# Weighted aggregation of a graph-attention layer: own rows added to source rows before the segment product

## The reference

```python
s_all = jnp.concatenate([src, loops])
d_all = jnp.concatenate([dst, loops])
...
alpha = p / z[d_all]
agg = jax.ops.segment_sum(alpha[:, :, None] * v[s_all], d_all, num_segments=n)
agg = jnp.where(deg[:, None, None] > 0, agg, jnp.zeros_like(agg))
att = agg.reshape(n, NH * HD) @ Wo + bo
x = residual + att
```

## Time and profile before

| | us |
|---|---|
| median of 3 runs (2486.36 to 2490.35) | 2487.27 |
| span of the profiled execution | 2872.0 |
| of it, the stage `weighted` | 365 (from 1745 to 2110) |
| TensorE busy | 2193.6 |
| VectorE busy | 1930.2 |
| ScalarE busy | 1328.2 |
| GpSimd busy | 1228.6 |

### The profile page before, as it was taken

How to read it: one execution, slowest core, us unless ns; L and a number is a source line. 1 busy time by engine, 2 the same in 40 slices (tenths; PEclk the granted TensorE clock), 3 DMA queues, 4 the chain that set the end, 5 groups by cost and what they waited for, 6 DMA issues and landing times. The chain is left out here.

```text
span 2872.0 us, 49421 instructions
## 1 busy us (share of the span) xinstructions
PE 2193.6 (76%) x14363; PEld 1777.0 (62%) x14363; DVE 1930.2 (67%) x7755; ACT 1328.2 (46%) x3166; POOL 1228.6 (43%) x1416
## 2 busy tenths in 40 slices
PE   2478777548887677728888806878849999999998
PEld 2355555348887566715656606777737777777776
DVE  3589999736665577736666694444547777777775
ACT  0489999712222244436656600000015656656655
POOL 3544434146652666445455103555543333333332
PEclk9789999879998899958888857888969999999999
DMA  3478888668775466624333104445432333333331
GB/s 92 133 213 244 243 239 250 178 184 232 232 229 175 125 197 199 185 94 119 110 119 117 58 9 116 131 145 153 130 123 83 106 111 104 106 111 102 108 111 49
DMA packets 354022, 413.95 MB, mean 144 GB/s; under 512 B 51578, under 2 KB 235278, under 8 KB 353754
## 3 DMA queue, kind: packets, MB, share of 16 engines
q1 hardware_dynamic: 316186, 340.50, 37.9%
q0 software_dynamic: 34496, 69.37, 9.1%
q10 hardware_dynamic: 3072, 0.92, 0.1%
HBM read 264.11 MB, written 179.90 MB: 155 GB/s over the span
## 5 line engine op out<-in xcount | busy, mean ns | idle before, releaser
L1746 PEld LDWEIGHTS p_y<-w,g_T 128*128 128x128 f32 x3136 | 365.4, 192 | 46.4 <-issue 24.2
L1746 PE MATMUL p_y<-w,g_T 128*128 128x128 f32 x3136 | 365.8, 275 | 0.0
L1764 ACT ACTIVATE nT<-p_n 128x512 f32<-128x512 f32 x98 | 58.5, 597 | 644.8 <-PE p_n L1754 644.8
L1739 PE MATMUL p_f<-nT,w 128*128 128x512 f32 x784 | 354.4, 595 | 0.0
L548 POOL DMA_INDIRECT x_dst<-in_x_dram,idx x196 | 189.0, 964 | 283.0 <-DMA edge_x<-x_dst 200.4
L1729 POOL TENSOR_TENSOR rstd<-var,minus_half 128x4 f32<-128x4 f32 x98 | 113.4, 1157 | 450.1 <-ACT res L1777 450.0
L1771 ACT ACTIVATE g_T<-p_f,bf 128x512 f32<-128x512 f32 x392 | 267.1, 681 | 31.5 <-PE p_f L1739 31.4
L1131 POOL DMA_INDIRECT x_src<-x_rows,idx x196 | 185.1, 944 | 210.5 <-ACT normed L1219 113.9
L1550 POOL DMA_INDIRECT x_rows<-xv,idx x196 | 197.3, 1007 | 160.5 <-DVE xv L1636 104.4
L902 POOL DMA_INDIRECT h_src<-h_table,idx x196 | 192.4, 982 | 156.2 <-POOLq L123 57.2
L894 POOL DMA_INDIRECT e_h<-in_x_dram,idx x172 | 168.3, 979 | 178.8 <-DVE msg L1010 78.4
(11 more groups left out here) (309 smaller groups left out, 5874.0 us busy)
## 6 DMA issues: line engine op xcount, KB each, us to landing
xs<-x_rows SPq DMA_DIRECT2D x98, 512.0 KB, 3.6
x_in<-in_x_dram SPq DMA_DIRECT2D x98, 256.0 KB
h_table<-h_rows SPq DMA_DIRECT2D x98, 256.0 KB
x_rows<-x_in SPq DMA_DIRECT2D x98, 256.0 KB, 2.9
out_dram<-res SPq DMA_DIRECT2D x98, 256.0 KB, 2.1
x_rows<-x_rows SPq DMA_DIRECT2D x50, 500.0 KB
edge_x<-x_dst SPq DMA_DIRECT2D x98, 128.0 KB
h_own<-edge_x SPq DMA_DIRECT2D x49, 256.0 KB
```

Of the source, the lines that this page charges most:

```text
L1739: e.matmul(p_f[ch][:], w_1[:, ch * P:(ch + 1) * P], nT[:, g % 2, :], start=True, stop=True).then_inc(f_prod, 1)
L1746: mm = e.matmul(p_y[g % 2][:, a * D:(a + 1) * D], g_T[:, g % 2, ch, a * P:(a + 1) * P], w_2[:, ch, :], start=(ch == 0), stop=(ch == FCH - 1))
```

## The change

The own rows are added to the source rows before the segment product, so one product of a tile does for two: the four identity products of a group are gone. VectorE gets a new addition for each group, `w_sum` plus `w_own`, both in SBUF, with a semaphore `weight_ready` of its own. An own row now goes through `mate` too and reaches every column of its segment, and through the carries the next tiles; so it must count once in a segment, and its weight is multiplied by `end_t` in place of `done_t`: 1 at the last edge of a segment alone. `end_t` is a value that `prepare` made before without keeping it, and is written to a tile of its own.

The carries move from lag 4 to lag 5, `p_out` from lag 5 to lag 6, the last sum from lag 6 to lag 7; OUT goes from AHEAD + 4 to AHEAD + 5, so there is one step more. Loads, scatters and the numbers of buffers stay.

```diff
-                    chain(e.tensor_tensor(tmp[:], tmp[:], real[:], ALU.mult))
-                    chain(e.scalar_tensor_tensor(out=tmp[:], in0=dst_f[:], scalar=-float(SKIP), in1=tmp[:],
+                    chain(e.tensor_tensor(end_t[:], tmp[:], real[:], ALU.mult))
+                    chain(e.scalar_tensor_tensor(out=tmp[:], in0=dst_f[:], scalar=-float(SKIP), in1=end_t[:],
...
-                    chain(e.tensor_tensor(top[:], top[:], over_heads(done_t), ALU.mult))
+                    chain(e.tensor_tensor(top[:], top[:], over_heads(end_t), ALU.mult))
...
-                OUT = AHEAD + 4
+                OUT = AHEAD + 5
...
                         if at_step(n, AHEAD + 1):
                             g = n - AHEAD - 1
-                            e.wait_ge(src_ready, g + 1)
                             e.wait_ge(mate_ready, g + 1)
-                            e.wait_ge(own_ready, g + 1)
+                            e.wait_ge(weight_ready, g + 1)
                             wait(e, attT_ready, GT * (g - 1))
                             for j in range(GT):
                                 at = slice(j * P, (j + 1) * P)
-                                e.matmul(p_att[g % 2][:, at], w_src[:, g % 2, j, :], mate[:, g % 2, at], start=True, stop=False)
-                                mm = e.matmul(p_att[g % 2][:, at], w_own[:, g % 2, j, :], ident[:], start=False, stop=True)
+                                mm = e.matmul(p_att[g % 2][:, at], w_sum[:, g % 2, j, :], mate[:, g % 2, at], start=True, stop=True)
...
-                        if at_step(n, AHEAD + 2):
-                            g = n - AHEAD - 2
+                        if at_step(n, AHEAD + 3):
+                            g = n - AHEAD - 3
...
+                    for n in range(STEPS):
+                        carried, weighed = at_step(n, AHEAD + 2), at_step(n, AHEAD)
+                        if carried:
+                            carry(n - AHEAD - 2, 0)
...
+                        if weighed:
+                            e.wait_ge(own_ready, g + 1)
+                            e.wait_ge(src_ready, g + 1)
+                            e.tensor_tensor(w_sum[:, g % 2, :, :], w_sum[:, g % 2, :, :], w_own[:, g % 2, :, :], ALU.add).then_inc(weight_ready, 1)
+                        if at_step(n, AHEAD + 4):
+                            g = n - AHEAD - 4
```

More of the change, by code:

```diff
@@ L179, in gnn_program @@
         done_col = sb("done_col", [P, T])
-        done_t = sb("done_t", [Q, W])
+        end_t = sb("end_t", [Q, W])
         same_prev = sb("same_prev", [Q, W])
@@ L211, in prepare @@
                 seg_f = sb("seg_f", [Q, W], F32, c)
+                done_t = sb("done_t", [Q, W], F32, c)
                 norm_f = sb("norm_f", [Q, W], F32, c)
@@ L1466, in weighted @@
                 mate = sb("mate", [P, 2, GROUP], F32, c)
-                w_src = sb("w_src", [P, 2, GT, D], F32, c)
+                w_sum = sb("w_sum", [P, 2, GT, D], F32, c)
                 w_own = sb("w_own", [P, 2, GT, D], F32, c)
@@ L1490, in weighted @@
                 own_ready = sem("own_ready", c)
+                weight_ready = sem("weight_ready", c)
                 att_prod = sem("att_prod", c)
@@ L1596, in _ @@
                 def _(e):
-                    for n in range(STEPS):
[L1598 to L1629, removed]
-                                                seg_col[:, g * GT:(g + 1) * GT].rearrange("p (q c) -> p q c", q=2)
-                                                .unsqueeze(3).to_broadcast([P, 2, 2, P]), ALU.is_equal).then_inc(mate_ready, 1)
-                            if j == 3 and at_step(n, AHEAD + 3):
-                                g = n - AHEAD - 3
-                                e.wait_ge(out_prod, g + 1)
-                                e.wait_ge(xv_in[g % VN], 16 * (g // VN + 1))
-                                e.tensor_tensor(xv[:, g % VN, :, X2, :], p_out[g % 2][:].rearrange("p (j d) -> p j d", j=GT),
-                                                xv[:, g % VN, :, X1, :], ALU.add).then_inc(row_ready, 1)
@@ new lines, in carry @@
+                    def carry(g, j):
+                        t = g * GT + j
+                        at = slice(j * P, (j + 1) * P)
+                        e.wait_ge(att_prod, g + 1)
+                        wait(e, out_prod, g - 1)
+                        if t == 0:
+                            e.tensor_copy(attT[:, 0, at], p_att[0][:, at]).then_inc(attT_ready, 1)
+                            return
+                        e.wait_ge(attT_ready, t)
+                        s, end = (t - 1) // GT % 2, (t - 1) % GT * P + P - 1
+                        e.scalar_tensor_tensor(out=attT[:, g % 2, at], in0=tile_row(rows[:, g % RN, :, :], j, FROM_PREV - SEG),
+                                               scalar=attT[:, s, end:end + 1], in1=p_att[g % 2][:, at],
+                                               op0=ALU.mult, op1=ALU.add).then_inc(attT_ready, 1)
```

27 lines of the change are left out of this document (added).

## The result

The change makes the kernel slower by a little: 2491.26 us (median of 6 runs, 2486.76 to 2497.22) against 2486.82 us of the kernel before (6 runs beside them). The ratio is 1.0023, with a 95% interval of 1.0013 to 1.0033, so +5.7 us, between 3 and 8. A repeat beside other kernels gave 1.0021 (1.0011 to 1.0030). The forecast of 2486 us, no measurable change, had the range right and the sign wrong.

A forecast was written before the change was run, and what follows sets the result against it. The prediction took GpSimd's scatters to bound the stage `weighted`, so removed products and added work were worth 0; 2487.3 - 1.5 + 1 = 2486.8, put at 2486 us, with a range of 2462 to 2500.

The forecast's parts named there:

- What sets the pace: In stage `weighted`, GpSimd's scatters set the timed stage, at about 280 us; chance 0.62.
- The budget of stages: Timed total less the other stages' floors leaves 263 to 306 us for `weighted`; GpSimd's own floor there is 278.
- the 15 long waits: VectorE's carries in `weighted` wait 93.5 us in 15 long pieces; mostly late completions belonging to the profiled execution.
- The step prices: Per group in `weighted`: GpSimd 5.16 us; TensorE 4.98 falling to 4.08; VectorE 3.4 rising to 4.0.
- the loop: In `weighted`, `mate`, `p_att`, carry 0 and back to `mate` take 4.98 us; as rival pacing the stage, 2469 us, chance 0.24.
- cover: GpSimd's 5.16 us a step hides TensorE's saving in `weighted`: worth 0, or 44 us if not hidden.
- The fill: From first `w_own` to first last sum, 17.8 us becomes 16.2: -1.5 us, bounds -3 and +5.
- the short steps: At the start of `weighted`: 3.6 us until the first addition is done, then 2.4, then three of 3.4.
- The 0.8 for an earlier backlog: From 2486.8 down to 2486: a late `p_att` at the start, before GpSimd has a backlog, delays it less.
- The holds: VectorE's new two-SBUF-input addition delays scatters starting shortly after it, up to 0.53 us each: +1 us, bounds -4 and +26.
- The second rival: A scatter held behind `mate` or the addition in every group, 0.3 us each: 2502 us, at most 2513; chance 0.12.
- The cold clock: TensorE, less busy, drops to its lower clock in `weighted`: up to 147 us more, 2634 us; chance 0.02.

The follow-up runs named there:

- e1: The kernel before, profiled and timed once more with no edit; ratio 1.0002 to the kernel before, profiled span 2483.4 us.
- e9: The kernel before with two scatters for each group in place of four (output not the reference's); 2461.79 us, ratio 0.9898.
- e10: The changed kernel with two scatters for each group in place of four (output not the reference's); 2419.49 us, ratio 0.9734.
- e3: The kernel before with carries, `p_out` and last sum one step later, both products kept and no addition; ratio 1.0005 to the kernel before.
- e2: The changed kernel with the weighted own rows kept in PSUM, so the addition has one SBUF and one PSUM input; 2487.8 us, ratio 1.0008.
- e7: The changed kernel with one more VectorE addition per step, ahead of the last sum, with two SBUF inputs; 2501.94 us, ratio 1.0068.
- e11: The changed kernel with own rows and `mate`'s segment numbers in PSUM, one PSUM tile for `p_out`, three `attT` buffers; 2481.8 us, ratio 0.9983.
- e8: The changed kernel with one more VectorE addition per step, ahead of the last sum, with one SBUF and one PSUM input; 2495.46 us, ratio 1.0034.
- e5: The changed kernel with own rows and `mate`'s segment numbers in PSUM, one PSUM tile for `p_out`, two `attT` buffers; 2518.43 us, ratio 1.0126.
- e12: As the changed kernel with own rows in PSUM, one `p_out` tile and three `attT` buffers, but `mate` reading segment numbers from SBUF; 2487.47 us, ratio 1.0004.

## Why the prediction was right and wrong

**What sets the pace: right.** The budget of stages left 263 to 306 us for `weighted`, with a floor of 278. In e1 the stage takes 18 us to the first last sum, 1.5 to the first scatter, 255.5 for the run and about 3 to land. That the 15 long waits would not be in timed executions was right too, and for the reason given. That they would come back in the profile after was wrong: its span was to be 2786 to 2819 and is 2489.4.

**The step prices: right in number, the loop wrong.** TensorE's 4.98 and 4.08 us a step are the spacings of `mate` in e1 (4.98) and at the start of the changed kernel (4.08 to 4.09). The 44 us that the removed products would be worth without cover are 42.3 in e9 and e10. With the cover they are worth nothing, as predicted; and so is the addition's own time. But the prediction took 4.98 us for a loop of `mate`, `p_att` and carry 0 that the change cuts. TensorE had been working without a pause (e1), and with the loop cut alone the step stayed at 4.98 us (e3). VectorE waited for `p_att` because it was the faster of the two. The sum was spared this error, because it took TensorE's own time for the step after.

**The fill: right in sign, small.** -1.5 was predicted and 17.3 against 17.7, -0.4, is what the profiles show; the last of the short steps, put at 3.4 us each, took 4.60. The 0.8 for an earlier backlog is not to be seen: GpSimd waited in the middle of the stage for 3 us at most before.

**The holds: the term that failed.** The mechanism was there, with its place and its largest price (0.53 us a hold; 1470 ns at most, 0.48, was seen in the changed kernel). Its size was put at +1 us, and it measured +4.3 in one profile and +5.7 in the other. With it the sum is -0.4 + 4.3 to 5.7, so +4 to +5, and the measured ratio says +5.7 with an interval of 3 to 8. Two thoughts of that step were at fault.

The first took `mate`'s own hits as given and looked only at the addition. But TensorE's step of 4.98 us had kept `mate` in a rhythm that held a scatter only in every fifth group. At 4.08 us a step it held one in ten groups in a row, and e2, with no hits of the addition at all, has 25 of `mate`'s instead of 10.

The second put the addition's hits at few because a group is rarely hit twice and the rhythm may lock at a good place. No group was hit twice, but 34 of 49 were hit once in place of 10. The rhythm did lock, for ten groups, and not at a good place: each `mate` cost 0.22 us. Once the loads waited for scatters, the lock broke, and the addition met 11 scatters, 14 in the repeat. Scatters of more than 1.2 us, of which the prediction wanted 10 to 15, are 20, and 23 in the repeat.

An estimate from rows that were at hand comes near. A hold is 0.56 us less the time by which the scatter starts after the instruction. If the starts fall evenly over the 1.29 us between scatters, the mean is 0.56 x 0.56 / (2 x 1.29) = 0.12 us, about 6 us for 49 instructions of one kind. So a second kind costs some 6 us, and the 4 us of before were below the average of one kind. The rule of the Trainium skill, taken for every group, would have made it 33 us; the trace has a hit in 34 of 98 such instructions, of 0.25 us on average. The second rival was thus the right one in kind, at a third of its price.

**The cold clock: not seen.** TensorE's granted clock in the run of scatters is 0.93 after the change and 0.91 in the repeat, against 0.95 in e1; the first profile had 0.87 for the stage.

**Chances.** Slower by over 0.2% had 0.17. The measured 0.23% lies just beyond that bound, and its interval on both sides of it. The range held.

Left open: why the stage of the first profile had late completions at all, since no run here brought them back; and why e7's timed runs stand some 4 us above what its profile accounts for. How the loss divides between `mate` and the addition rests on the profiles; e2's time alone can't tell it.

## What to carry to other kernels

Work taken off an engine that is not the slowest gains nothing, but it changes the rhythm at which that engine's instructions meet those of the slowest one; where the two share something, count the meetings again, for the old instructions as well as the new; if the rhythm can't be foretold, the mean over all phases is a better guess than the hits of the old rhythm. Here GpSimd issued the indirect DMAs that set the pace, and each VectorE instruction with two SBUF inputs was a possible hold: moving one operand to PSUM (e2, e11) took it away at no cost in VectorE's time. And when a profile's span lies far above the timed runs, take the profile again before reading waits from it, or at least check each wait against a budget of the stages.

## What the runs showed of the hardware

A scatter of GpSimd that starts 0.02 to 0.55 us after the start of a VectorE instruction with two SBUF inputs (0.68 us long) takes 1.0 to 1.53 us where others take 0.985. Wherever in this stretch it starts, it ends 1.54 us after the start of the VectorE instruction, within 0.02 us, which is 0.86 us after its end; the two pairs of lines above, at 1462.97 and 1467.05, show it. This holds for all such scatters of `weighted` in the profiles here, but for those held by two instructions, and none that started 0.02 to 0.52 us behind such an instruction went free. A scatter that starts before the instruction is not held. Within 0.02 us behind it most are not (in e1 six started up to 0.012 us after a `mate` and took 0.99 us), but one in e8 is. Two such instructions in a row hold one scatter for both, up to 2.12 us in e7; in the changed kernel a carry, with one tensor input in PSUM, stands between `mate` and the addition, and no scatter took more than 1.47 us. With one of the inputs in PSUM no hold was seen behind the instruction (e2, e5, e8, e11). VectorE's own instructions stayed at 0.68 us, and took up to 0.74 us only where `mate` and a scatter started within some 0.02 us of each other, so it is nearly always GpSimd that pays.

That this is a lock held for the whole instruction is what the Trainium skill says (SBUF — State Buffer, "Who interferes with whom"), and the trace agrees for the scatter that comes second: its end hangs on the end of VectorE's instruction alone, and e11 against e12 shows the worth of one operand's place, 5.7 us. That whichever comes second is blocked in full is not borne out for VectorE: `mate` took 0.68 us behind a scatter that had started 0.05 to 0.96 us before.

The profiles of one kernel, before, differed by 388.6 us of span (2872.0 and 2483.4), with the same instructions and the same timed medians within 0.1%.
